# Softmax attention on one core: two heads as two half-height matmul tiles, maxima as four block-diagonal rows, sums packed into quarter tiles

## What is computed

```python
q = split_heads(x @ Wq.T); k = split_heads(x @ Wk.T); v = split_heads(x @ Wv.T)
sim = jnp.einsum('bhid,bhjd->bhij', q, k) * DIM_HEAD ** -0.5
m = jnp.max(sim, axis=-1, keepdims=True)
e = jnp.exp(sim - m)
attn = e / (jnp.sum(e, axis=-1, keepdims=True) + 1e-10)
out = jnp.einsum('bhij,bhjd->bhid', attn, v)
return out.transpose(0, 2, 1, 3).reshape(B, N, 1024) @ Wo.T + bo
```

## Time and profile before

| what | value |
|---|---|
| median of three runs | 2222.82 us (2221.43 to 2230.84) |
| the profiled execution | 2225.31 us, span 2223.6 us |
| attention stage, from the first score to the last output | about 269 to 1150 us of the span |
| busy share of the span | PE 72%, DVE 71%, POOL 46%, ACT 41% |
| granted TensorE clock, mean of the span | 0.882 |

### The profile page before, as it was taken

One profiled execution on the slowest core, in us unless ns is written; L12 is line 12 of the kernel. 1 busy time (PEld: TensorE's weight loads), 2 busy tenths in 40 slices (PEclk: granted clock), 3 DMA queues, 4 the chain that ended last, 5 costly groups with the idle time before them and its releaser, 6 DMA issues. The chain is left out here.

```text
span 2223.6 us, 29789 instructions
## 1 busy us (share of the span) xinstructions
PE 1599.6 (72%) x9139; PEld 934.4 (42%) x9139; DVE 1569.2 (71%) x3212; ACT 912.8 (41%) x2102; POOL 1028.3 (46%) x1332
## 2 busy tenths in 40 slices
PE   0546389999999999999965563158658888830686
PEld 0334134444444444444423343135437767730453
DVE  5887778878788888877878886336467777752563
ACT  0112255555555555555522221035336676610452
POOL 0111245555555555555532224635435555546353
PEclk9889599999999999999987895579879999955898
DMA  6000022222222222222200000122300000001224
GB/s 186 0 0 1 23 63 58 58 58 58 63 59 61 60 59 58 58 58 59 62 9 1 0 0 24 56 77 80 104 16 1 1 1 1 1 32 62 75 81 145
DMA packets 126010, 104.05 MB, mean 47 GB/s; under 512 B 19680, under 2 KB 120480, under 8 KB 125856
## 3 DMA queue, kind: packets, MB, share of 16 engines
q1 hardware_dynamic: 111616, 77.75, 13.6%
q0 software_dynamic: 8704, 18.89, 2.5%
q10 hardware_dynamic: 5536, 5.52, 0.8%
HBM read 29.32 MB, written 22.30 MB: 23 GB/s over the span
## 5 line engine op out<-in xcount | busy, mean ns | idle before, releaser
L770 ACT ACTIVATE at_pT<-at_turned 128x512 f32<-128x512 f32 x512 | 305.6, 597 | 290.3 <-PE at_turned L837 271.2
L669 DVE TENSOR_REDUCE at_nmax<-at_score 128x1 f32<-128x512 f32 x512 | 337.1, 680 | 69.8 <-PE at_score L814 66.8
L648 POOL TENSOR_TENSOR m_rows<-at_pT 128x512 f32<-128x512 f32 x128 | 162.5, 1269 | 375.1 <-ACT at_pT L770 375.1
L691 DVE RECIPROCAL m_rows<-m_rows 128x512 f32<-128x512 f32 x64 | 214.6, 3353 | 37.7 <-ACT m_rows L776 37.7
L875 PE MATMUL at_pv<-at_pT,at_v 128*64 128x512 f32 x1024 | 230.6, 592 | 0.0
L814 PE MATMUL at_score<-at_kh,at_both 128*128 128x512 f16 x512 | 196.7, 385 | 22.6 <-DVE at_nmax L669 17.0
L1056 POOL DMA_INDIRECT by_token<-m_ysb,m_dest x144 | 138.2, 960 | 144.7 <-DVE m_ysb L1136 109.5
L836 PE MATMUL at_turned<-at_both,at_kh 128*128 128x512 f16 x512 | 194.9, 381 | 0.4 <-ACT at_pT L770 0.3
L837 PE MATMUL at_turned<-at_both,at_kl 128*128 128x512 f16 x512 | 194.8, 380 | 0.0
L656 POOL TENSOR_TENSOR m_rows<-m_rows,at_pT 128x512 f32<-128x512 f32 x128 | 162.8, 1272 | 10.6 <-ACT at_pT L770 0.7
L652 POOL TENSOR_TENSOR m_rows<-m_rows,at_pT 128x512 f32<-128x512 f32 x128 | 162.7, 1271 | 10.4 <-ACT at_pT L770 0.5
(11 more groups left out here) (309 smaller groups left out, 3685.0 us busy)
## 6 DMA issues: line engine op xcount, KB each, us to landing
at_both<-at_part_q SPq DMA_DIRECT2D x128, 128.0 KB, 2.4
at_kh<-at_part_k SPq DMA_DIRECT2D x256, 64.0 KB, 2.0
m_xin<-by_expert SPq DMA_DIRECT2D x144, 72.0 KB
at_both<-at_part_q SPq DMA_DIRECT2D x128, 64.0 KB, 2.1
at_kl<-at_part_k SPq DMA_DIRECT2D x128, 64.0 KB
m_rows<-by_token SPq DMA_DIRECT2D x32, 256.0 KB, 4.8
by_token<-m_ysb,m_dest POOLq DMA_INDIRECT x144
m_x<-in_x SPq DMA_DIRECT2D x8, 256.0 KB, 4.7
```

The lines of the kernel that those rows point to most:

```text
L648: nc.gpsimd.tensor_tensor(acc, pT[g % 2][:, head, 0, :], pT[g % 2][:, head, 1, :], ALU.add).then_inc(chain, 1)
L669: nc.vector.tensor_reduce(nmax[head][:, qt:qt + 1], score[use % 2][:], AX.X, ALU.max, negate=True)\
L691: nc.vector.reciprocal(rinv, total).then_inc(rinv_done, 1)
L770: nc.scalar.activation(pT[g % 2][:, head, kt, :], turned[i % 2][:], ACT.Exp).then_inc(exp_done, 1)
```

## The change

Nothing is copied between halves any more. `high_of` and `low_of` hold the parts of q and k with each head on its own 64 rows, as the projection gives them. A score matmul uses 64 rows: head 0 the rows 0 to 63, head 1 the rows 64 to 127, one behind the other into two banks, and only of the high parts. The second pass has three such products for each head (high-high, high-remainder, remainder-high) and a fourth one that brings in the maxima: `nmax` has the four maxima columns of head 0 at column 0 and those of head 1 at column 32, one transposition gives rows 0 to 3 and 32 to 35, DVE spreads them with a mask `own` into a block diagonal `mdiag` of 4 rows x 512, and a matmul of four rows for each head (starting at rows 0 and 32) with a constant `unit` adds them. The ten transfers of `to_rows` and the two of `max_row` are gone.

The sums over keys are made in four tiles of 32 columns (two heads x two halves of the queries), so that 128x256 numbers hold all of them; ACT and DVE work on 256 instead of 512 columns, and SP spreads the inverse to the 128x512 layout by eight transfers of 32 rows x 1 KB. The value products are issued in four parts between the other work, and the pipeline is one period longer: `normalise` is done for pair g-2, `output` for pair g-3 and v's projection for pair g in period g. The order of the lists on PE, ACT, DVE and POOL is by key tile (both heads of tile 0, both heads of tile 1, ...) instead of by head.

```diff
-        both = [s.sb(f"both{i}", [P, 2, 2, SEQ], F16) for i in range(RING)]
-        kh = [s.sb(f"kh{i}", [P, 2, SEQ], F16) for i in range(RING)]
-        kl = [s.sb(f"kl{i}", [P, 2, SEQ], F16) for i in range(RING)]
-        part = [s.sb(f"part_{n}", [P, 2, SEQ], F16) for n in "qk"]
+        HALF = SEQ // 2
+        QUAD = P // 4
+        high_of = [[s.sb(f"high_{n}{i}", [P, SEQ], F16) for i in range(RING)] for n in "qk"]
+        low_of = [[s.sb(f"low_{n}{i}", [P, SEQ], F16) for i in range(RING)] for n in "qk"]
...
-        total, rinv = mem["w_attn"][:, 2, 0:SEQ], mem["w_attn"][:, 2, SEQ:2 * SEQ]
-        nmax = [s.sb(f"nmax{i}", [P, P]) for i in range(2)]
-        mrow = [s.sb(f"mrow{i}", [TPB, P], F16) for i in range(2)]
+        total, packed, rinv = mem["w_attn"][:, 2, 0:HALF], mem["w_attn"][:, 2, HALF:SEQ], mem["w_attn"][:, 2, SEQ:2 * SEQ]
+        nmax = s.sb("nmax", [P, 2 * QUAD])
+        own = s.sb("own", [2 * QUAD, TPB])
+        mdiag = s.sb("mdiag", [2 * QUAD, TPB, P], F16)
+        unit = s.sb("unit", [2 * QUAD, P], F16)
...
+        max_bank = sums[0:2 * QUAD, HALF:HALF + P]
...
-                def to_rows(g, which, part_i):
-
-                    src = part[which]
-                    k = g % RING
+                for g in range(PAIRS_ALL):
+                    sp.wait_ge(packed_done, g + 1)
+                    if g:
+                        sp.wait_ge(o_done, g)
                     for head in range(2):
-                        rows = src[halves[head], part_i, :]
-                        if which == 0 and part_i == 0:
-                            sp.dma_start(both[k][0:DH, :, head, :], rows.unsqueeze(1).to_broadcast([DH, 2, SEQ])).then_inc(s_in[k], 16)
-                        elif which == 0:
-                            sp.dma_start(both[k][DH:P, 0, head, :], rows).then_inc(s_in[k], 16)
-                        elif part_i == 0:
-                            sp.dma_start(kh[k][0:DH, head, :], rows).then_inc(s_in[k], 16)
-                            sp.dma_start(kh[k][DH:P, head, :], rows).then_inc(s_in[k], 16)
-                        else:
-                            sp.dma_start(kl[k][0:DH, head, :], rows).then_inc(t_in[k], 16)
...
-                    sp.dma_start(both[g % RING][DH:DH + 1, 1, head, :].rearrange("o (t q) -> o t q", q=P), mrow[head][:])\
-                      .then_inc(m_in[head], 16)
...
+                        for half in range(2):
+                            first = (2 * head + half) * QUAD
+                            for to in (head * DH, head * DH + QUAD):
+                                sp.dma_start(rinv[to:to + QUAD, half * HALF:(half + 1) * HALF], packed[first:first + QUAD, :])\
+                                  .then_inc(rinv_in, 16)
...
+                    for kt in range(1, TPB):
+                        for head in range(2):
+                            acc = psum[g % 2][:, head, :]
+                            before = pT[g % 2][:, head, 0, :] if kt == 1 else acc
...
+                def max_rows(g):
+                    dve.wait_ge(m_done, g + 1)
                     if g:
+                        dve.wait_ge(t_done, 8 * g)
+                    wide = [2 * QUAD, TPB, P]
+                    nc.vector.tensor_tensor(mdiag[:], max_bank.unsqueeze(1).to_broadcast(wide), own[:].unsqueeze(2).to_broadcast(wide),
+                                            ALU.mult).then_inc(m_out, 1)
...
+                def invert(g):
                     dve.wait_ge(total_done, g + 1)
-                    nc.vector.reciprocal(rinv, total).then_inc(rinv_done, 1)
+                    if g:
+                        dve.wait_ge(rinv_in, 16 * R_DMAS * g)
...
+                    nc.vector.reciprocal(packed, total).then_inc(packed_done, 1)
...
+                    dve.wait_ge(rinv_in, 16 * R_DMAS * (g + 1))
...
-                for i in range(RING):
-                    nc.vector.memset(both[i][DH:P, 1, :, :], 0.0)
-                    nc.vector.memset(kl[i][DH:P, :, :], 0.0).then_inc(set_up, 1)
-                nc.vector.memset(ones[:], 1.0).then_inc(set_up, 1)
-                dve.wait_ge(set_up, RING + 2)
-                for i in range(RING):
-                    last = nc.vector.memset(kl[i][DH:DH + 1, :, :], M_UNIT)
-                last.then_inc(set_up, 1)
+                nc.vector.memset(unit[:], M_UNIT)
+                nc.vector.memset(ones[:], 1.0)
+                nc.vector.tensor_tensor(own[:], mem["ident"][0:2 * QUAD, 0:TPB], mem["ident"][0:2 * QUAD, QUAD:QUAD + TPB], ALU.add)\
+                  .then_inc(set_up, 1)
...
-                    nc.scalar.activation(total, sums[:], ACT.Copy, bias=SM_EPS).then_inc(total_done, 1)
+                    nc.scalar.activation(total, sums[:, 0:HALF], ACT.Copy, bias=SM_EPS).then_inc(total_done, 1)
...
-                    nc.tensor.matmul(score[use % 2][:], both[k][:, 0, head, qt * P:(qt + 1) * P], kh[k][:, head, :], start=True,
-                                     stop=True).then_inc(s_done, 1)
+                def scores(g, qt):
+                    if qt == 0:
+                        pe.wait_ge(hi_done, 2 * g + 2)
+                    if g or qt:
+                        pe.wait_ge(s_read, 8 * g + 2 * qt)
+                    for head in range(2):
+                        rows = halves[head]
+                        nc.tensor.matmul(score[head][:], high_of[0][g % RING][rows, qt * P:(qt + 1) * P], high_of[1][g % RING][rows, :],
+                                         start=True, stop=True).then_inc(s_done, 1)
+
+                def max_turned(g):
+                    pe.wait_ge(s_read, 8 * (g + 1))
+                    if g:
+                        pe.wait_ge(m_out, g)
+                    if g >= 2:
+                        pe.wait_ge(total_done, g - 1)
+                    nc.tensor.transpose(max_bank, nmax[:], mem["ident"][:]).then_inc(m_done, 1)
+
...
-                    nc.tensor.matmul(turned[i % 2][:], kh[k][:, head, tile], both[k][:, 0, head, :], start=True, stop=False)
-                    nc.tensor.matmul(turned[i % 2][:], kl[k][:, head, tile], both[k][:, 1, head, :], start=False, stop=True)\
-                      .then_inc(t_done, 1)
+                    for n, (k_of, q_of) in enumerate(((high_of, high_of), (high_of, low_of), (low_of, high_of))):
+                        for head in range(2):
+                            if n == 0 and (g or kt):
+                                pe.wait_ge(exp_done, 8 * g + 2 * kt + head - 1)
+                            rows = halves[head]
+                            nc.tensor.matmul(turned[head][:], k_of[1][k][rows, tile], q_of[0][k][rows, :], start=(n == 0), stop=False)
+                    if kt == 0:
+                        pe.wait_ge(m_out, g + 1)
+                    for head in range(2):
+                        rows = slice(head * QUAD, head * QUAD + TPB)
+                        nc.tensor.matmul(turned[head][:], unit[rows, :], mdiag[rows, :, :].rearrange("p t q -> p (t q)"), start=False,
+                                         stop=True).then_inc(t_done, 1)
...
+                            first = (2 * head + half) * QUAD
+                            last = nc.tensor.matmul(sums[first:first + QUAD, 0:HALF], ones[:],
+                                                    psum[g % 2][:, head, half * HALF:(half + 1) * HALF], start=True, stop=True)
...
+                    for kt in range(TPB):
+                        if live(g):
+                            scores_turned(g, kt)
                         if live(g + 1):
-                            scores(g + 1, i)
-                        if live(g):
-                            scores_turned(g, i)
-                        if i == 1 and live(g):
-                            max_turned(g, 1)
-                        if i == 2 and live(g + 2):
-                            project(g + 2, 0)
-                        if i == 3:
-                            if live(g - 2):
-                                output(g - 2)
+                            scores(g + 1, kt)
+                        if kt == 0:
+                            if live(g + 2):
+                                project(g + 2, 0)
+                            if live(g - 3):
+                                output(g - 3)
+                        elif kt == 1 and live(g - 1):
+                            add_up(g - 1)
+                            values(g - 1, 0)
+                        elif kt == 2:
                             if live(g + 2):
                                 project(g + 2, 1)
+                            if live(g - 1):
+                                values(g - 1, 1)
+                        elif kt == 3:
+                            if live(g - 1):
+                                values(g - 1, 2)
                             if live(g + 1):
-                                max_turned(g + 1, 0)
+                                max_turned(g + 1)
                             if live(g - 1):
-                                values(g - 1)
```

(52 more changed lines are left out.)

203 lines of the change are left out of this document (69 added, 134 removed).

## The result

The changed kernel takes 2249.6 us, median of four runs (2247.04 to 2250.06), against 2224.31 for the kernel before (four runs): ratio 1.0107, 95% interval 1.0083 to 1.0132. It is slower by 1.1%. The forecast was 2246 in a range of 2165 to 2315.

The account below looks back on a forecast made before the run. PE bounds the attention stage; a pair is 11.15+2.15+0.59 = 13.89 us instead of 13.46, +27 us over 62 pairs, and the ends -3: 2225.3+27-3 = 2249, less 2.5 to the median, forecast 2246, range 2165 to 2315.

Parts of the forecast that it names:

- What bounds the stage: Attention stage: PE sets the pace, busy 847.7 of 885 us; DVE, ACT and POOL come nowhere near.
- Streaming work: PE's matmul time per pair: 12.55-1.40 = 11.15 us, from cheaper scores, sums and one transposition less.
- Price of a change: Each tile-shape change on PE: 0.104 us into row tiles or whole array, 0.147 into column tiles with 32-bit weights.
- Rival 1: Row heights switch freely on PE: 2170 us, chance 0.16; only 64 to 32 rows free: 2195, chance 0.14.
- Number of changes: Tile-shape changes on PE: 19 a pair instead of 2, costing 2.15 us.
- last doubt: The 64-column transposition might run as a whole-array one: two more changes, +0.15 a pair, +9 us.
- The wait: PE waits 0.59 us a pair before transposing the maxima, for DVE's last two maxima.
- The ends: Start and end of the attention stage: together -3 us.
- Set-up: Stage start: five small instructions replace DVE's set-up while PE waits, -6 us (from -7.5 to 0).
- Ramp: Stage start: the first scores' 1.7 us wait for a transfer goes, -2 us (to -4).
- Tail: Stage end: shorter last inversion, but 7.1 us of transfers ahead of the last normalisation, +5 us (4 to 7).
- The transfers of the inverse: Eight new SP transfers between inversion and normalisation cost nothing, with 2 us to spare.

Follow-up runs that it names:

- one half at a time: Changed kernel with head 1's three products held by a semaphore until head 0's last is done; 2483.6 us, ratio 1.1149 to the kernel before.
- 8 changes fewer: Changed kernel with the maxima added by zero-padded 64-row matmuls instead of 32-row tiles; 2120.03 us on another chip, ratio 0.9862 to the kernel before.
- 3 fewer: Changed kernel with the 32-row maxima matmuls issued before the 64-row products for key tiles 1 to 3; 2228.15 us against 2248.36.

## Why the prediction was right, point by point

- **What bounds the stage: right.** PE, before and after. Halving the inversion and dropping twelve transfers a pair did not shorten the steady part (they were not tried alone), and each run's time moved with PE's shapes, slots and its one wait.
- **Streaming work, 11.15 us: right.** Slots of 0.22 in the half tiles, and the sums down from 0.86 to about 0.43. The reason held also: one half at a time costs +3.46 a pair.
- **Price of a change, 0.104 for row tiles, taken from the nearest row: right.** 0.10 by the steps of the changed kernel, by 8 changes fewer (-0.79; the two around the transposition, which the expectation called new, stood there already) and by 3 fewer (-0.31). Rival 1 at 0.30 together was the real danger, and no row of before could exclude it. The Trainium skill, TensorEngine Tiling (Array Packing), Key Properties, says that changing the mode drains the engine; the steps of 0.31 and 0.32 agree with it.
- **Number of changes, 19: too few.** The transposition of 64 columns behaves as a whole-array instruction, so there are 21. The text had this as its last doubt, +0.15 a pair; the second of the two is paid, the first is hidden in the wait. The middle pair is 714.46-700.43 = 14.03 us by the output instructions instead of 13.89:

```profile
700.43 1.05 PE L835 MATMUL at_out<-m_woT,at_oT 128*128 128x128 f32 x8
714.46 0.27 PE L835 MATMUL at_out<-m_woT,at_oT 128*128 128x128 f32 x1
```

- **The wait, 0.59: right.** Between the end of the value products (708.94+1.08-0.165 = 709.86) and the transposition lie 0.53, which hide the change of shape. Removing it gave -0.67 together with the change behind the transposition.
- **The ends, -3: the sum was off, -7.** Set-up: -6 said; PE's first projection came 0.9 instead of 7.5 after DVE's first instruction, -6.6. Ramp: -2 said, -4.9 measured (the rest of -11.5). The term counted the first scores' wait for a transfer, 1.68, and left out the second pair's, 2.48, which is gone as well. Together 4.2 of the 4.9. Tail: +5 said, +4.5 measured.

```profile
280.53 0.61 PE L814 MATMUL at_score<-at_kh,at_both 128*128 128x512 f16 x1 [2.48 <-DMA at_kh<-at_part_k]
```

- **By luck:** the pairs were 0.09 to 0.14 dearer than said and the start 3.5 cheaper. +28.6-7.0 = +21.6 against the +27-3 = +24 of the forecast. The errors of the two terms, +1.6 and -4.0, have opposite signs, and part of the closeness of 2246 to the measured 2249.6 is owed to that.
- **The transfers of the inverse, free: right in the steady part.** There the eight are issued by 705.89+5.15 = 711.04 and land 1.8 us later at the median, and the normalisation that needs them starts at 715.18: 2.3 us to spare, where 2 were said. They are waited for only in the last three pairs: 1.50 here, then the 6.95 and 6.28 of the rows at the end of the stage.

```profile
705.89 5.15 SPq L596 DMA_DIRECT2D m_rows<-m_rows  x8
715.18 0.68 DVE L655 TENSOR_TENSOR at_oT<-at_pv,m_rows 128x512 f32<-128x512 f32 x1
1146.62 0.69 DVE L655 TENSOR_TENSOR at_oT<-at_pv,m_rows 128x512 f32<-128x512 f32 x1 [1.50 <-DMA m_rows<-m_rows]
```

## What to carry to other kernels

Count the changes of tile shape before packing small matmuls: at 0.10 to 0.15 us each, two around a slot of 0.22 double its price. Here a tile padded with zero rows to its neighbours' height was cheaper than the tile that just fits (-0.79 a pair), and an odd-shaped matmul was cheaper at the border between two other shapes (-0.31). Put an instruction that needs another engine's last result behind everything that doesn't need it.

## What the runs showed of the hardware

- The two 64-row tiles take up their instructions independently: three instructions of head 0 ahead of three of head 1 still ran in pairs (13.98 against 13.91 us a pair). The order of issue decides little, a semaphore decides much (17.37).
- Four 32-bit tiles of 32 columns run side by side as well as two of 64 (eight instructions in a record of 1.04, four in 1.03 before).
- A 32-bit transposition into 64 partitions, shown as 128*64, behaves as a whole-array instruction: 0.10 behind 64-column products, and no change before the whole-array projection (710.43 and 710.57).
- A change of tile shape costs 0.10 us with 16-bit weights, of row height too (8 fewer: -0.79 a pair; 3 fewer: -0.31), and the weight load behind it is held back until its own matmul can start (702.16 for 702.17).
- The kernel before took 2149.56 us on one chip and 2224 to 2228 on two others, while the changed kernel's pairs were 13.91 on both of the latter. The 79 us lie in the two expert stages: from the last matmul of the feed-forward layer to the first of the linear attention 294.9 us in the changed kernel against 254.6 in the kernel with 64-row maxima, and from the last of the linear attention to the end of the span 278.5 against 239.0. Why the expert stages differ is open.
